# A graph network's gathered rows and one-hots in fp32: two products a tile instead of six, and 56 columns instead of 64

## The chip, the cores and the metric

The kernel runs on one core of one Trainium2 chip. The metric is the device time of one execution in microseconds. Three runs of the kernel before are shown, and one more that was taken with the hardware profiler.

## The reference

The kernel computes two relational graph convolutions over 6250 nodes with 256 features and 206250 edges, then a choice of a linear layer by node type, then a mixture of experts. What the change touches is the first part, twice:

```python
W = jnp.einsum('rb,bde->rde', comp, basis)      # 8 relations from 4 bases
h = jnp.einsum('nd,rde->nre', x, W)
msg = h[src, edge_type]
seg = dst * R + edge_type                        # R = 8
sums = segment_sum(msg, seg, n * R)
cnt = segment_sum(ones, seg, n * R)
agg = (sums / max(cnt, 1)).reshape(n, R, -1).sum(axis=1)
return agg + x @ root + bias                     # relu behind it
```

The edges come sorted by their destination. The input of the first layer is the layer norm of x. Behind the second layer stand `x + lin_w[node_type] ...`, a second layer norm, and 8 experts (256 to 512 to 256, GELU, the two best of eight weighted by a softmax), added to x.

## The kernel before, in words

The kernel does not multiply each edge's message by W. It sums the source rows of each (node, relation) first and multiplies the sums afterwards. A block is 64 nodes, which is 512 (node, relation) columns; there are 98 blocks, 49 pairs. The edges of a block are cut into 18 tiles of 128 (TILES). For a tile, POOL gathers the 128 source rows from a table in DRAM into a slot (L558, an indirect DMA, one slot for each of the 18 tiles), DVE makes a one-hot of each edge's column (L929), and TensorE multiplies the gathered rows (stationary, 128 x 128) by the one-hot (moving) into PSUM banks S[0] and S[1], one for each half of the 256 features (L1251). In the first layer a product of ones by the one-hot counts the edges of each column in bank C (L1247).

**Three parts.** To keep fp32 accuracy with bf16 products the tables hold each row as three bf16 numbers (PARTS = 3: a rounded value, the rounded remainder, and the remainder of that), so a row has 3 x 256 bf16 values, 1536 bytes, and a tile needs 2 halves x 3 parts = 6 products. The one-hot and the ones are bf16, too. Making the parts is work of its own. In the setup, group_parts (L793 to L797) on DVE and a copy on ACT (L636) make them for the first table, in 7 groups of 7 x 128 nodes; store_group on SP (L389 to L395) writes them. In the first layer, save (L955 to L960) on DVE and publish (L669 to L678) on ACT make them for the second table, from the transposed result in T2.

**Columns of a tile.** As the edges are sorted, a tile's edges fall in a few neighbouring nodes. A tile writes SPAN = 8 nodes, COLS = 64 columns, from its base on. The base is the tile's first node, but no more than the base of the tile before plus COLS and no more than TOP = 512 - COLS (L818 to L821). Bases travel to TensorE packed four to a word (L1237 to L1243). If an edge falls outside its tile's columns, `general_i` is set (L842 to L861) and a general path is run instead, which takes 128 edges a step, 1612 steps a layer, with an indirect gather and an indirect adding scatter in each.

**Order of the work.** Everything is written out by hand, engine by engine, with semaphores.

- Setup: SP loads the edges and x in groups (load_group, L347); DVE finds the windows, makes statistics (group_stats, L770), ACT normalizes (norm_group, L622: seven operations L630, then the rounding L636), TensorE transposes each group (turn_group, L1139) and ACT copies it to featT (L643). POOL starts its gathers when all stores of the first table have landed (L603, L604).
- Layer 1: POOL gathers tile after tile, for all pairs; each third tile it waits until TensorE has released the slots (`used`, L569). TensorE takes a block's 18 tiles; after an even block it runs transform of the pair before (L1269: 20 fp32 products of root and bases), after an odd block turn (L1288: 2 transposes, 4 fp32 products). DVE divides by the counts and scales (scale, L933), mixes the bases (mix_bases, L901), makes the next one-hots, and saves. A block's first tile waits for the scaling of the block before (sc_ready, L1220).
- Between the layers: POOL waits until all of the second table has landed (L613).
- Layer 2: TensorE's stream is one list, dense() (L1356), which interleaves the experts of pair r (up, L1338; down, L1351), transform and typed products (L1311, L1312) of pair a, and the tiles of pair y's second block and pair x's first block, one or two tiles at a place. A product of the router (L1328) has 8 columns.

A fp32 product is one call in the code and shows as two matmul records in the trace, each with a weight load; a bf16 product, and a transpose, is one.

Of the kernel before, what the change touches and what calls it, by code (L numbers as in the profile page):

```python
# [14 lines left out]
P = 128  # L15
# [22 lines left out]
PARTS = 3  # L38
# [8 lines left out]
SPAN = 8  # L47
# [21 lines left out]
def build(nc, x, src, dst, etype, ntype, basis0, comp0, root0, bias0, basis1, comp1, root1, bias1,  # L69
          lin_w, lin_b, gamma, beta, Wr, br, W1, b1, W2, b2, out):  # L70
    with ExitStack() as ctx:
# [12 lines left out]
        table = [dram("table0", (NPAD, PARTS * D), BF16), dram("table1", (NPAD, PARTS * D), BF16)]  # L84
# [9 lines left out]
        slot = sb("slot", [P, TILES, PARTS * D], BF16)  # L94
# [18 lines left out]
        ones_b = sb("ones_b", [P, P], BF16)  # L113
# [10 lines left out]
        parts = sb("parts", [P, PARTS, D], BF16)  # L124
        rest = sb("rest", [P, D], F32)
# [25 lines left out]
        def carve(t, at, n):  # L151
            return t[:, at:at + n]
# [3 lines left out]
        grest = carve(ffn_w, 4 * GW, GW).rearrange("p (t d) -> p t d", t=GROUP)  # L156
        gparts = [carve(ffn_w, 5 * GW + i * PARTS * GW // 2, PARTS * GW // 2).bitcast(BF16).rearrange(
            "p (t q d) -> p t q d", t=GROUP, q=PARTS) for i in range(2)]
# [6 lines left out]
        early = slot[:, :, :].rearrange("p t d -> p (t d)").bitcast(F32)  # L165
# [6 lines left out]
        idx_all = carve(ffn_w, 5 * GW + PARTS * GW, BLOCKS * TILES).bitcast(I32).rearrange(  # L172
# [23 lines left out]
        g_rows = carve(early, 3 * MW, PARTS * D // 2).bitcast(BF16)  # L196
        g_sum = carve(early, 3 * MW + 384, MCOLS)
        same = carve(early, 3 * MW + 648, P // 2).bitcast(BF16)
# [57 lines left out]
        g_hi = sem("g_hi")  # L256
        g_rest = sem("g_rest")
        g_mid = sem("g_mid")
        g_lo = sem("g_lo")
# [15 lines left out]
        rest_done = sem("rest_done")  # L275
        mid_done = sem("mid_done")
        lo_done = sem("lo_done")
        parts_out = sem("parts_out")
# [59 lines left out]
        def _(sp):  # L338
# [3 lines left out]
            for q in (sc_ready, relu_done, rest_done, b2_added, mid_done, lo_done, znT_done, lin_acc, feat_saved, *used.values()):  # L342
                sp.sem_inc(q, START)
# [162 lines left out]
            with sp.If(general):  # L506
                sp.wait_ge(parts_out, 16 * PAIRS)
                general_sums(1)
# [977 lines left out]
```

## Time and profile before

| | us |
|---|---|
| median of 3 runs | 4842.9 (4841.66 to 4844.88) |
| the profiled execution | 4840.02 |
| its span, first to last instruction | 4838.2 |
| mean granted TensorE clock, share of full | 0.782 |
| TensorE busy | 3842.3 (79%) |
| TensorE weight loads busy | 3300.8 (68%) |
| DVE busy | 3017.5 (62%) |
| ACT busy | 881.8 (18%) |
| POOL busy | 3331.7 (69%) |

The span holds setup up to about 178 us, layer 1 up to about 2360 us and layer 2 with the experts after it. A busy share is the part of the span in which an instruction of the engine was running; an engine at 69% can still be the one that sets the pace, if the rest is its own time between instructions ("issue"). Matmuls overlap, so their pace is read from start to start and not from the duration of one. The granted clock has two levels, 1.2 GHz (0.5) and 2.4 GHz (1.0).

### The profile page before, as it was taken

How to read it: one execution, taken by the hardware profiler on the slowest of the kernel's cores; microseconds unless marked ns; L12 is line 12 of the kernel's file. 1: busy time of each engine (PE TensorE's matmuls, PEld its weight loads, DVE VectorE, ACT ScalarE, POOL GpSimd, SP SyncE). 2: the span in 40 equal slices, each digit the busy share in tenths (PEclk: the TensorE clock that was granted, in tenths of full speed). 3: DMA queues.
4: the chain of work that ended last, by engine and by line, in shares of the span. 5: the costliest groups of instructions: out<-in, count | busy, mean ns of one | idle time of the engine just before them, and what ended most of it. 6: DMA issues, size and time to landing. Idle time of an engine off the chain costs nothing.

```text
span 4838.2 us, 119647 instructions
## 1 busy us (share of the span) xinstructions
PE 3842.3 (79%) x38119; PEld 3300.8 (68%) x38120; DVE 3017.5 (62%) x6579; ACT 881.8 (18%) x2470; POOL 3331.7 (69%) x3374
## 2 busy tenths in 40 slices
PE   1366666666666666666469999999999999999999
PEld 1255555555555555555358888888888888888888
DVE  4556656666666566666456666666666666666663
ACT  1200000000000000000013333333333333333333
POOL 0477777777777777777477676767676777676770
PEclk6555555555555555555569999999999999999999
DMA  4656655555555555555465555555555555555551
GB/s 129 192 171 183 176 158 156 157 158 158 155 157 159 156 157 158 158 156 157 117 169 166 156 159 155 158 154 158 154 158 156 158 157 160 154 160 154 159 158 22
DMA packets 344661, 749.10 MB, mean 155 GB/s; under 512 B 128323, under 2 KB 167806, under 8 KB 344430
## 3 DMA queue, kind: packets, MB, share of 16 engines
q0 software_dynamic: 215040, 662.09, 48.7%
q1 hardware_dynamic: 115510, 70.49, 5.6%
q10 hardware_dynamic: 14076, 16.04, 1.0%
q8 instruction: 23, 0.38, 0.0%
q14 instruction: 12, 0.10, 0.0%
HBM read 719.00 MB, written 29.35 MB: 155 GB/s over the span
## 4 chain that ended last, share of the span: by engine, by line
PE 59%; issue 12%; DVE 12%; POOL 9%; DMA 8%; DVEq 0%; SPq 0%; ACT 0%; POOLq 0%; ACTq 0%
PE bank L1351 15%; PE bank L1338 14%; PE bank L1251 11%; POOL slot L558 9%; PE bank L1283 8%; DMA slot<-table,idx 6%; DVE inv L939 4%; PE bank L1247 3%; DVE scaled L945 3%; PE bank L1311 3%; PE bank L1312 2%; DVE mixed L913 2%; PE bank L1279 1%; DVE inv L938 1%; PE bank L1314 1%
## 5 line engine op out<-in xcount | busy, mean ns | idle before, releaser
L558 POOL DMA_INDIRECT slot<-table,idx x3354 | 3326.0, 992 | 1342.0 <-issue 1085.2
L1251 PE MATMUL bank<-hot,slot 128*128 (+1 forms) x21168 | 1380.1, 212 | 67.5 <-DMA slot<-table,idx 60.6
L1251 PEld LDWEIGHTS bank<-hot,slot 128*128 128x128 bf16 x21168 | 1112.1, 108 | 219.4 <-issue 75.0
L1247 PE MATMUL bank<-hot,ones_b 128*128 x1764 | 398.7, 226 | 745.4 <-DMA slot<-table,idx 340.1
L1338 PE MATMUL bank<-xnT,ffn_w 128*128 128x128 f32 x6272 | 867.1, 285 | 20.0 <-DVE scaled L945 20.0
L1247 PEld LDWEIGHTS bank<-hot,ones_b 128*128 128x128 bf16 x1764 | 181.0, 103 | 1006.4 <-issue 969.2
L1351 PE MATMUL bank<-ffn_w,act 128*128 128x256 f32 x3136 | 842.0, 395 | 0.3 <-DVE o L1024 0.3
L1338 PEld LDWEIGHTS bank<-xnT,ffn_w 128*128 128x128 f32 x6272 | 755.8, 192 | 46.4 <-DVE scaled L945 28.8
L1351 PEld LDWEIGHTS bank<-ffn_w,act 128*128 128x128 f32 x3136 | 541.1, 191 | 60.7 <-issue 16.9
L913 DVE SCALAR_TENSOR_TENSOR mixed<-scaled,small,mixed 128x256 f32<-128x256 f32 x1372 | 573.7, 480 | 12.2
L913 DVE SCALAR_TENSOR_TENSOR mixed<-scaled,comp_sb,mixed 128x256 f32<-128x256 f32 x1372 | 573.5, 480 | 10.5
L938 DVE TENSOR_SCALAR inv<-bank 128x512 f32<-128x512 f32 x98 | 67.5, 688 | 778.9 <-PE bank L1251 778.9
L691 ACT ACTIVATE act<-bank,small 128x128 f32<-128x128 f32 x1568 | 442.9, 373 | 582.1 <-PE bank L1338 580.9
L1283 PE MATMUL bank<-mixed,basis_sb 128*128 128x128 f32 x3136 | 474.7, 311 | 0.0
L1283 PEld LDWEIGHTS bank<-mixed,basis_sb 128*128 128x128 f32 x3136 | 454.2, 228 | 0.0
L945 DVE TENSOR_TENSOR scaled<-bank,inv 128x512 f32<-128x512 f32 x392 | 377.5, 1040 | 65.8 <-PE bank L1251 52.4
L939 DVE RECIPROCAL inv<-inv 128x512 f32<-128x512 f32 x98 | 328.6, 3353 | 3.4
L1024 DVE SCALAR_TENSOR_TENSOR o<-bank,wfull,o 128x256 f32<-128x256 f32 x343 | 164.5, 480 | 250.3 <-PE bank L1351 245.2
L929 DVE TENSOR_TENSOR hot<-iota_b,rel 128x1152 bf16<-128x1152 bf16 x196 | 264.8, 1352 | 47.1 <-DMA off<-off_d 31.8
L665 ACT ACTIVATE hcur<-bank,small 128x128 f32<-128x128 f32 x98 | 30.7, 364 | 1120.7 <-PE bank L1283 1029.3
L691 ACT ACT_TABLE_LOAD x96 | 123.2, 1283 | 348.4 <-DVE o L1024 347.5
L988 DVE SCALAR_TENSOR_TENSOR x<-bank,tmask,x 128x256 f32<-128x256 f32 x196 | 94.8, 484 | 128.2 <-PE bank L1312 128.2
(148 smaller groups left out, 2192.0 us busy)
## 6 DMA issues: line engine op xcount, KB each, us to landing
slot<-table,idx POOLq DMA_INDIRECT x3354, 3.1
inv<-inv_d SPq DMA_DIRECT2D x98, 256.0 KB, 3.8
table<-ffn_w SPq DMA_DIRECT2D x7, 1344.0 KB, 6.0
table<-parts ACTq DMA_DIRECT2D x49, 192.0 KB, 3.1
ffn_w<-in_L_ffn_W_dram SPq DMA_DIRECT2D x16, 512.0 KB
xcur<-in_x_dram SPq DMA_DIRECT2D x48, 128.0 KB
out_dram<-o ACTq DMA_DIRECT2D x48, 128.0 KB
ffn_w<-in_x_dram SPq DMA_DIRECT2D x6, 896.0 KB, 9.0
```

The costliest lines, as they stand in the source:

```text
L558: gp.indirect_dma_start(out=slot[:, k, :], out_offset=None, in_=table[layer], in_offset=bass.IndirectOffsetOnAxis(ap=idx[:, h, k:k + 1], a ...
L691: last = sc.activation(act[:, e % 2, c, :], HP[e % 2][:, c * P:(c + 1) * P], ACT.Gelu, bias=b1_sb[:, e * HCH + c:e * HCH + c + 1])
L913: ins = v.scalar_tensor_tensor(out=mixed[:, b, :, :], in0=scaled[:, :, r, :], scalar=s, in1=mixed[:, b, :, :], op0=ALU.mult, op1=ALU.add)
L929: v.tensor_tensor(hot[:, h, :, :], iota_b[:, :].unsqueeze(1).broadcast_to([P, TILES, COLS]), rel[:, h, :].unsqueeze(2).broadcast_to([P, TI ...
L939: ch.link(v.reciprocal(iv, iv))
L945: last = v.tensor_tensor(scaled[:, k, :, h * BD:(h + 1) * BD].rearrange("p r n -> p n r"), S[k][:, :].rearrange("p (n r) -> p n r", r=R), ...
L1024: v.scalar_tensor_tensor(out=o[:, :], in0=YP[e % 2][:, 0:D], scalar=wfull[:, 0, e:e + 1], in1=acc[:, :], op0=ALU.mult, op1=ALU.add).then_i ...
L1247: t.matmul(C[:, at], ones_b[:, :], oh, start=(k == 0), stop=(k == TILES - 1), skip_group_check=True)
L1251: last = t.matmul(S[f][:, at], slot[:, k, q * D + f * P:q * D + (f + 1) * P], oh, start=(k == 0 and q == 0), stop=(k == TILES - 1 and q == ...
L1283: last = t.matmul(T[:, o_ * P:(o_ + 1) * P], basis_sb[:, b, k, o_ * P:(o_ + 1) * P], mixed[:, b, k, :], start=(layer == 1 and n == 1), sto ...
L1338: last = t.matmul(HP[e % 2][:, c * P:(c + 1) * P], w1_sb[:, e, k, c * P:(c + 1) * P], xnT[:, k, :], start=(k == 0), stop=(k == HALVES - 1))
L1351: last = t.matmul(YP[e % 2][:, 0:D], act[:, e % 2, c, :], w2_sb[:, e, c, :], start=(c == 0), stop=(c == HCH - 1))
```

## The change

The tables hold plain fp32 rows of 256 values (1024 bytes), and the gathered rows, the one-hots and the ones are fp32. A tile needs one product a half, two in all, and the count product in layer 1. Nothing is split into parts any more: group_parts goes, with ACT's rounding, the store waits for the norm alone and sends xn; save loses its two subtractions, publish is one copy. The norm waits on ACT for the landing of the store two groups before, ahead of its seven operations and no longer behind them. turn waits for `hi_done` (ACT has copied T2) and not for the remainder. SPAN is 7, so a tile has 56 columns and TOP is 456.

```diff
-PARTS = 3
-SPAN = 8
+SPAN = 7
...
-        table = [dram("table0", (NPAD, PARTS * D), BF16), dram("table1", (NPAD, PARTS * D), BF16)]
+        table = [dram("table0", (NPAD, D), F32), dram("table1", (NPAD, D), F32)]
...
-        slot = sb("slot", [P, TILES, PARTS * D], BF16)
+        EARLY = TILES * 384
+        early = sb("early", [P, EARLY], F32)
+        slot = early[:, 0:TILES * D].rearrange("p (t d) -> p t d", t=TILES)
...
-        iota_b = sb("iota_b", [P, COLS], BF16)
+        iota_c = sb("iota_c", [P, COLS], F32)
-        hot = sb("hot", [P, 2, TILES, COLS], BF16)
+        hot = sb("hot", [P, 2, TILES, COLS], F32)
...
             def store_group(i, g):
-                sp.wait_ge(g_hi, g + 1)
-                sp.wait_ge(g_mid, g + 1)
-                sp.wait_ge(g_lo, g + 1)
+                sp.wait_ge(g_norm, g + 1)
...
-                sp.dma_start(dst_ap, gparts[i].rearrange("p t q d -> p t (q d)")).then_inc(g_out[i], 16)
+                sp.dma_start(dst_ap, xn[i]).then_inc(g_out[i], 16)
...
                     act_.wait_ge(g_Tc, g - 1)
-                    act_.wait_ge(g_rest, g - 1)
+                    act_.wait_ge(g_out[i], 8 * (g - i))
...
-                act_.wait_ge(g_norm, g + 1)
-                if not isinstance(g, int) or g >= 2:
-                    act_.wait_ge(g_out[i], 8 * (g - i))
-                sc.activation(gparts[i][:, :, 0, :], xn[i], ACT.Copy).then_inc(g_hi, 1)
...
             def publish(p):
                 act_.wait_ge(hT_done, p + 1)
-                act_.wait_ge(parts_out, p * 16)
-                sc.activation(parts[:, 0, :], T2[:, 0:D], ACT.Copy).then_inc(hi_done, 1)
-                act_.wait_ge(rest_done, START + p + 1)
-                sc.activation(parts[:, 1, :], rest[:, :], ACT.Copy).then_inc(mid_done, 1)
-                act_.wait_ge(lo_done, START + p + 1)
-                act_.wait_ge(mid_done, START + p + 1)
+                act_.wait_ge(rows_out, p * 16)
+                sc.activation(turned[:, :], T2[:, 0:D], ACT.Copy).then_inc(hi_done, 1)
+                act_.wait_ge(hi_done, START + p + 1)
...
-            def group_parts(i, g):
-
-                dve.wait_ge(g_hi, g + 1)
-                if not isinstance(g, int) or g >= 1:
-                    dve.wait_ge(g_lo, g)
-                v.tensor_tensor(grest, xn[i], gparts[i][:, :, 0, :], ALU.subtract).then_inc(g_rest, 1)
-                dve.wait_ge(g_rest, g + 1)
-                v.tensor_copy(gparts[i][:, :, 1, :], grest).then_inc(g_mid, 1)
-                dve.wait_ge(g_mid, g + 1)
-                v.tensor_tensor(gparts[i][:, :, 2, :], grest, gparts[i][:, :, 1, :],
-                                ALU.subtract).then_inc(g_lo, 1)
...
                               ROOTED[:, 0:D].rearrange("p (k n) -> p k n", k=HALVES)).then_inc(feat_saved, 1)
-                dve.wait_ge(hi_done, p + 1)
-                dve.wait_ge(mid_done, START + p)
-                dve.wait_ge(lo_done, START + p)
-                v.tensor_tensor(rest[:, :], T2[:, 0:D], parts[:, 0, :], ALU.subtract).then_inc(rest_done, 1)
-                dve.wait_ge(mid_done, START + p + 1)
-                v.tensor_tensor(parts[:, 2, :], rest[:, :], parts[:, 1, :], ALU.subtract).then_inc(lo_done, 1)
...
                     if self.layer == 0:
-                        t.matmul(C[:, at], ones_b[:, :], oh, start=(k == 0), stop=(k == TILES - 1),
+                        t.matmul(C[:, at], ones_f[:, :], oh, start=(k == 0), stop=(k == TILES - 1),
                                  skip_group_check=True)
                     for f in range(HALVES):
-                        for q in range(PARTS):
-                            last = t.matmul(S[f][:, at],
-                                            slot[:, k, q * D + f * P:q * D + (f + 1) * P], oh,
-                                            start=(k == 0 and q == 0), stop=(k == TILES - 1 and q == PARTS - 1),
-                                            skip_group_check=True)
+                        last = t.matmul(S[f][:, at], slot[:, k, f * P:(f + 1) * P], oh, start=(k == 0),
+                                        stop=(k == TILES - 1), skip_group_check=True)
...
             def turn(p):
                 pe.wait_ge(relu_done, START + p + 1)
-                pe.wait_ge(rest_done, START + p)
+                pe.wait_ge(hi_done, START + p)
```

The rest of the diff renames (`parts_out` to `rows_out`), drops the buffers and semaphores of the parts, and does the same to the general path. It is left out.

## Rows read from the trace of the kernel before

**Rows 1.** Windows of both layers: busy us (instructions) by engine, granted clock, DMA share, GB/s.

```profile
178.00:2360.00 2182.00, 1442.28 (x14748) 1162.54 (x14748) 1365.36 (x2166) 68.05 (x191) 1658.98 (x1674) 0.58 0.57 160
2510.00:4800.00 2290.00, 2269.75 (x22347) 2030.09 (x22345) 1480.19 (x3981) 741.56 (x2108) 1572.33 (x1586) 1.00 0.55 153
```

**Rows 2.** Groups by line, 1000 to 2000 us: busy us, mean ns, idle before.

```profile
L558 POOL DMA_INDIRECT slot<-table,idx x772 | 765.0, 991 | 235.2 <-issue 202.9 <-PE bank L1251 27.4 <-DMA off<-off_d 4.9
...
L1247 PE MATMUL bank<-hot,ones_b 128*128 x810 | 183.0, 226 | 326.3 <-DMA slot<-table,idx 143.1 <-DVE scaled L945 88.3 <-issue 77.5
```

**Rows 3.** Timeline of TensorE, layer 1: start us, us, line, operation.

```profile
1064.07 0.66 PE L1292 MATMUL bank<-ident,hcur 128*128 128x128 f32 x2
...
1506.11 0.66 PE L1292 MATMUL bank<-ident,hcur 128*128 128x128 f32 x2
...
1512.37 0.23 PE L1247 MATMUL bank<-hot,ones_b 128*128 x1 [3.89 <-DVE scaled L945]
...
1528.07 1.92 PE L1283 MATMUL bank<-mixed,basis_sb 128*128 128x128 f32 x8
1529.78 0.49 PE L1279 MATMUL bank<-featT,root_sb 128*128 x2
1530.10 1.06 PE L1283 MATMUL bank<-mixed,basis_sb 128*128 128x128 f32 x8
1530.99 0.39 PE L1279 MATMUL bank<-featT,root_sb 128*128 x2
```

**Rows 4.** Timeline of TensorE, layer 2.

```profile
3016.49 1.89 PE L1351 MATMUL bank<-ffn_w,act 128*128 128x256 f32 x8
3018.22 0.51 PE L1328 MATMUL bank<-wr_sb,xnext 128*128 128x8 f32 x4
3018.66 0.38 PE L1329 MATMUL bank<-br_sb,ones_f 1*128 1x8 f32 x2
3018.97 1.16 PE L1338 MATMUL bank<-xnT,ffn_w 128*128 128x128 f32 x8
3019.97 0.34 PE L1251 MATMUL bank<-hot,slot 128*128 128x64 bf16 x6
3020.14 1.14 PE L1338 MATMUL bank<-xnT,ffn_w 128*128 128x128 f32 x8
3021.11 0.51 PE L1251 MATMUL bank<-hot,slot 128*128 128x64 bf16 x12
3021.46 1.11 PE L1351 MATMUL bank<-ffn_w,act 128*128 128x256 f32 x4
3022.41 0.34 PE L1251 MATMUL bank<-hot,slot 128*128 128x64 bf16 x6
```

**Rows 5.** Windows of one pair in layer 1, cut where the clock changed.

```profile
1489.02:1495.85 6.83, 5.57 (x75) 4.62 (x75) 2.02 (x2) 0.63 (x2) 5.37 (x5) 1.00 0.51 142
1495.85:1533.40 37.55, 24.67 (x246) 19.86 (x245) 26.50 (x44) 0.80 (x2) 28.65 (x30) 0.55 0.57 160
```

**Rows 6.** Groups by line, whole run: a gather in the setup.

```profile
L553 POOL DMA_INDIRECT slot<-key_d,start_i x1 | 1.0, 972 | 10.1 <-DVE start_i L807 10.1
```

**Rows 7.** Timeline of DVE and ACT, setup.

```profile
108.48 0.42 DVE L776 BATCH_NORM_STATS2 gstats<-ffn_w 128x6 f32<-128x256 f32 x1 [3.96 <-issue]
...
149.06 0.42 DVE L776 BATCH_NORM_STATS2 gstats<-ffn_w 128x6 f32<-128x256 f32 x1 [0.66 <-issue]
...
156.65 1.70 ACT L636 ACTIVATE ffn_w<-ffn_w 128x1792 bf16<-128x1792 f32 x1
...
163.30 2.03 DVE L797 TENSOR_TENSOR ffn_w<-ffn_w 128x1792 bf16<-128x1792 f32 x1
```

**Rows 8.** Chain that ended last, in order of time, setup: start us, us.

```profile
165.41 5.51 DMA table<-ffn_w
```

More of the change, by code:

```diff
@@ L123, in build @@
         hcur = sb("hcur", [P, HALVES, P], F32)
-        parts = sb("parts", [P, PARTS, D], BF16)
-        rest = sb("rest", [P, D], F32)
+        turned = sb("turned", [P, D], F32)
         xcur = sb("xcur", [P, D], F32)
@@ L195, in build @@
         zeros = carve(early, 2 * MW, MW)
-        g_rows = carve(early, 3 * MW, PARTS * D // 2).bitcast(BF16)
+        g_rows = carve(early, 3 * MW, D)
         g_sum = carve(early, 3 * MW + 384, MCOLS)
-        same = carve(early, 3 * MW + 648, P // 2).bitcast(BF16)
+        same = carve(early, 3 * MW + D, P)
         below = carve(early, 3 * MW + 712, P)
@@ L274, in build @@
         hi_done = sem("hi_done")
[L275 to L278, printed above, removed]
+        rows_out = sem("rows_out")
         inv_out = sem("inv_out")
@@ L341, in _ @@
             sp.sem_inc(out_done, 16 * START)
-            for q in (sc_ready, relu_done, rest_done, b2_added, mid_done, lo_done, znT_done, lin_acc, feat_saved, *used.values()):
+            for q in (sc_ready, relu_done, hi_done, b2_added, znT_done, lin_acc, feat_saved, *used.values()):
                 sp.sem_inc(q, START)
@@ L607, in _ @@
                 general_sums(0)
-                gp.wait_ge(parts_out, 16 * PAIRS)
+                gp.wait_ge(rows_out, 16 * PAIRS)
                 general_sums(1)
@@ L862, in _ @@
             v.memset(idle[:, :], 0.0).then_inc(tables_ready, 1)
-            group_parts(0, 0)
             ch0 = ch.n - 2 * GL
@@ L869, in _ @@
                     group_stats(i, g2 * 2 + i)
-                    group_parts(1 - i, g2 * 2 + i - 1)
             ch.begin(ch0 + GL * (GROUPS - 1))
             group_stats(0, GROUPS - 1)
-            group_parts(1, GROUPS - 2)
-            group_parts(0, GROUPS - 1)
             general = is_general(dve)
@@ L1189, in general_sums @@
                     pe.wait_ge(edge_rows, n * 16 + 16)
-                    t.matmul(T2[:, D:MCOLS], same, ones_b[:, 0:1], start=True, stop=True)
-                    for q in range(PARTS):
-                        last = t.matmul(T2[:, 0:D], same, g_rows[:, q * D:(q + 1) * D], start=(q == 0),
-                                        stop=(q == PARTS - 1))
+                    t.matmul(T2[:, D:MCOLS], same, ones_f[:, 0:1], start=True, stop=True)
+                    last = t.matmul(T2[:, 0:D], same, g_rows, start=True, stop=True)
                     last.then_inc(edge_sum, 1)
@@ L1246, in tile @@
                     if self.layer == 0:
-                        t.matmul(C[:, at], ones_b[:, :], oh, start=(k == 0), stop=(k == TILES - 1),
+                        t.matmul(C[:, at], ones_f[:, :], oh, start=(k == 0), stop=(k == TILES - 1),
                                  skip_group_check=True)
                     for f in range(HALVES):
-                        for q in range(PARTS):
-                            last = t.matmul(S[f][:, at],
-                                            slot[:, k, q * D + f * P:q * D + (f + 1) * P], oh,
-                                            start=(k == 0 and q == 0), stop=(k == TILES - 1 and q == PARTS - 1),
-                                            skip_group_check=True)
+                        last = t.matmul(S[f][:, at], slot[:, k, f * P:(f + 1) * P], oh, start=(k == 0),
+                                        stop=(k == TILES - 1), skip_group_check=True)
                     if k % RUN == RUN - 1:
```

22 lines of the change are left out of this document (6 added, 16 removed).

## The prediction

> **What bounds the kernel now.** I read the windows first, to cut the run into its stages, then the waits inside each, then the order of TensorE's work at the scale of one tile. Layer 1 (178 to 2360 us) and layer 2 (2510 to 4800 us) have different limits [rows 1]. In layer 1 TensorE is busy 1442 of 2182 us at a mean granted clock of 0.58, in layer 2 for 2270 of 2290 us at 1.00. So layer 2 is TensorE's: whatever is added to its stream there is added to the time.
>
> In layer 1 the engine that is always at work is POOL. Over 1000 us it issued 772 gathers; each shows 991 ns, and of the 235 us between them 203 end in "issue", that is, in nothing but its own sequencer; 27 us are waits for TensorE. TensorE meanwhile waits for gathered rows or for DVE (326 us ahead of the count product L1247) [rows 2]. A gather each 1.25 us is POOL's pace, and a pair of blocks (some 34 gathers) takes 44.2 us: (1506.11 - 1064.07) / 10 from one turn (L1292) to the tenth after it [rows 3].
>
> **What one product costs.** This decides the case, so I read it from start to start in the timeline. At full clock a bf16 tile of layer 2 is six products of 64 columns, and from its first one to the next dense product is 3020.14 - 3019.97 = 0.17 us: 0.029 each. Twelve take 0.35 us. There is a hidden bill behind them: the four records L1351 after a double tile take 3022.41 - 3021.46 = 0.95 us where their own pace, 1.73 us for eight (L1351, 3016.49 to 3018.22), makes it 0.87 [rows 4]; so each switch from tile to dense costs 0.08 more, since there are no long columns left to load fp32 weights behind. A tile alone thus costs 0.25 us, a double one 0.43.
>
> An fp32 product is two records in this trace, each with a weight load of its own. Its pace with 128 columns is 0.89 / 8 = 0.111 us at full clock (L1283, 1530.10 to 1530.99) [rows 3]. The row that bears on the change is L1328: fp32 weights of 128 by 128, and only 8 columns. Its four records still need 3018.66 - 3018.22 = 0.44 us, 0.110 each [rows 4]. So from 8 to 128 columns the weight load sets the pace and the columns cost nothing; 56 columns lie in between. Cutting the span from 64 to 56 columns then buys TensorE nothing. At the half clock the same 128-column record takes (1529.78 - 1528.07) / 8 = 0.214 us [rows 3], and I take a weight-bound record to double likewise.
>
> The six bf16 loads at 0.029 us each are what the old form has going for it. The Trainium skill, "TensorE: Matmul & The Clock Gate", section on LDWEIGHTS, prices any load by its columns alone, at 1.2 a nanosecond. By that estimate six loads of 128 would cost 0.64 us a tile and four 0.43, and layer 2 would win 36 x 0.21 x 46.5 = 350 us. The rows have 0.17 us for the six, so the measurement decides. The page's own next section exempts weights that are not fp32, and that exemption is what the change gives up.
>
> **Part by part.**
>
> Layer 2, tiles: six bf16 records become four fp32 ones: 4 x 0.110 = 0.44 us, and the next dense weight load is already one of the intervals counted. A single tile gains 0.44 - 0.25 = 0.19 us, a double one 0.88 - 0.43 = 0.45 us. By the calls in dense() a pair has 31 places: 26 single, 5 double (18 tiles in the block y, 18 in the block x). 26 x 0.19 + 5 x 0.45 = 7.2 us a pair; 46 loop passes and about half a pair after them: 46.5 x 7.2 = **+335 us**, all on the path, as TensorE has no idle time there. Lower bound: the columns' pace (see the third rival), -51 us. An upper end from loads and columns not overlapping is excluded by the 128-column rows.
>
> Layer 1, tiles: seven records become six (count, S0, S1, two each). The trace of before has no such stream, so I bound it. At half clock a tile takes 6 x 0.214 = 1.28 us, 36 tiles 46.2 us; transform's 40 records 8.6 us; and from the turn to the next block's first tile TensorE waits for DVE's division and scaling, 1512.37 - 1506.11 = 6.3 us, with turn inside [rows 3]. Together 61.1 us, more than POOL's 44.2: TensorE would become the bound here too. Each microsecond at full clock takes one off. Now the clock is full for 6.83 us a pair, after transform's run, then 37.55 us mostly at half, while the engine waits between tiles [rows 5]. If that stays, a pair takes 61.1 - 6.8 = 54.3 us. If the clock is full for 17 us or more, POOL binds again at 44.2, as all 36 tiles at full need only 36 x 0.66 = 23.8 us. What the clock does in a backlog of weight-bound products, where the engine never waits but streams its 56 columns in 56/128 of the time that a record of 128 takes, no row shows. It lies between the two things that rows do show: transform, columns without a break, after which the clock rose, and tiles with waits, after which it fell. I take the middle, 49.3 us, with full clock for 11.8 us: +5.1 x 48 pairs = **+245 us**; bounds 0 and +10.1 x 48 = +485.
>
> POOL's gathers move 1024 bytes a row, not 1536. I book nothing: the gather of 98 rows of 9.2 KB took 972 ns, that of 128 rows of 1.5 KB 991 [rows 2, 6], so bytes do not set it. The DMA share of 0.57 [rows 1] falls, which no one waits for.
>
> Setup: group_parts (three DVE operations of 2 us a group) and ACT's rounding copy go. Groups come 10.15 us apart now, (149.06 - 108.48) / 4. Without the parts a group is statistics, ACT's seven normalizing operations, transposes and copies in a ring, near 9 us; I take 1 us for each of four intervals. Behind the last group ACT begins its rounding at 156.65 with the norm done, yet the last part ends at 165.33 [rows 7]; that store can leave 8.7 us earlier, and its 5.51 us transfer [rows 8] shrinks by a third of its bytes, 1 us. Sum **-13 us**; bounds -18 and -5. ACT's norm now waits for the store of two groups before, ahead of seven operations, and the root of the next group and the featT copies queue behind it; that store is issued a whole group earlier and lands in 5.5, so nothing is booked. On SP the store waits for the norm alone and is sent sooner, ahead of the next loads, which also share the DMA engines: that is in the -5.
>
> Save and publish lose two DVE operations, an ACT one and their waits; turn waits for the copy out instead of the remainder. All lie beside POOL's stream, except once between the layers, less than two gathers' time: nothing booked. One-hots in fp32 have an eighth fewer columns on DVE, which is busy 1365 of 2182 us in layer 1 [rows 1]: nothing.
>
> **Sum.** 4838.2 - 13 + 245 + 335 = 5405; the profiled execution lies 1.8 us over its span (4840.0) and 2.9 under the median: 5410 us.
>
> **Rivals.**
>
> First, the clock in layer 1 stays as it is, 6.8 us a pair: 5410 + 240 = 5650 us. For it: the array is less in use per microsecond than in transform; the clock has fallen after every pair. Chance 0.3.
>
> Second, a TensorE that never waits gets the full clock until its backlog is gone: layer 1 keeps POOL's pace, 5410 - 245 = 5165 us. For it: both stretches after which it fell have waits for rows; layer 2 never loses it. Chance 0.28. The skill's same page, section on the clock gate, has it that activity releases a throttle that is the default; by it this rival's 5165 would come out, if loading weights counts as activity, which it does not say.
>
> Third, the other sign: the weight load of the second record is hidden, and 56 columns go at the columns' pace, (0.216 - 0.111) / 128 us a column, 0.052 us a record. A tile then takes 0.21 us with no switch bill: 0.04 less single, 0.01 less double, 1.1 us a pair, -51 us; layer 1 stays POOL's; with setup 5410 - 245 - 335 - 51 = 4779 us. It decides from 0.0625 us a record down (0.25 / 4). Against it: L1328's 0.110 with 8 columns. Chance 0.04. That page's table of back-to-back gaps would put up to 64 columns at its issue floor; the section warns that pairs of load and product go by both.
>
> Fourth, it does not do what it says: with 7 nodes an edge falls outside its tile's window and the whole kernel takes the general path, 1612 steps a layer with gathers and sums one behind another, tens of milliseconds. Counted over the reference's edges, the largest column any tile needs is 55 of 56 and all 206250 are matched. Under 0.01.
>
> **Chances.** Forecast 0.36, first 0.3, second 0.28, third 0.04, rest 0.02. The range goes from just under the second to just above the first: 5140 to 5690. A measurement of this kernel tells about 0.2% from no change; faster 0.04, same 0.01, slower 0.95.
>
> **What would show it.** Records of L1251 in layer 2 0.11 us apart, four to a tile, and a pair 7 us longer: right; 0.05 apart: the third. In layer 1 POOL's waits for TensorE instead of 27 us in a thousand: the first or the forecast, and the granted clock of the stretch tells them apart (about 0.56 for the first, 0.62 for mine, 0.69 and no waits for the second). Setup right if the first gather starts some 13 us earlier. An L558 much under 991 ns would prove my POOL term wrong.

## The result, and the profile after

The changed kernel takes 5568.9 us (median of 4 runs, 5534.9 to 5618.4) where the kernel before took 4843.9 beside it (4841.7 to 4845.9): a ratio of 1.147 (1.141 to 1.154), for which the highest run, over 1.5% above the lowest, is left out. The profiled execution of after is 5553.33 us, its span 5551.1, which is 712.9 us more than the span of before. The page of after has these two rows, of busy time and of the granted clock in 40 slices:

```profile
PE 5097.1 (92%) x32827; PEld 4895.5 (88%) x32828; DVE 2906.6 (52%) x6460; ACT 850.9 (15%) x2414; POOL 3313.7 (60%) x3373
...
PEclk7566665666666566676669999999999999999999
```

TensorE is busy 92% instead of 79%, though it has fewer records (32827 instead of 38119). The windows of after, for layer 1, for layer 2 and for 1000 us of layer 1 (columns as in [rows 1]), say in which stage TensorE sets the pace:

```profile
165.00:2800.00 2635.00, 2345.47 (x13108) 2310.11 (x13107) 1336.51 (x2113) 49.52 (x147) 1657.19 (x1695) 0.64 0.32 91
2900.00:5520.00 2620.00, 2602.98 (x18935) 2449.68 (x18934) 1461.02 (x3979) 738.95 (x2101) 1567.88 (x1574) 1.00 0.33 93
1000.00:2000.00 1000.00, 902.85 (x4993) 890.27 (x4993) 515.50 (x817) 19.16 (x57) 633.14 (x644) 0.63 0.31 88
```

In layer 1 TensorE went from 1442 of 2182 us busy [rows 1] to 2345 of 2635. Against [rows 2] the waits in the groups of 1000 to 2000 us have turned round:

```profile
L543 POOL DMA_INDIRECT early<-table,idx x644 | 633.1, 983 | 363.8 <-issue 181.1 <-PE bank L1203 179.3 <-DMA off<-off_d 3.4
L1203 PE MATMUL bank<-hot,early 128*128 x2696 | 622.1, 376 | 0.0
...
L1200 PE MATMUL bank<-hot,ones_f 128*128 x1347 | 378.0, 377 | 96.5 <-DVE scaled L906 95.5 <-issue 0.4
```

POOL issues 644 gathers instead of 772 and waits 179 us for TensorE where it waited 27. TensorE waits for gathered rows no more, only for DVE's scaling. A gather of 1024-byte rows shows 983 ns, one of 1536 bytes 991: bytes did not set it.

**Layer 2, one tile.** The timeline of TensorE after, in the stretch that answers to [rows 4], and the router's row over the whole run for both kernels (first and last of 49 pairs' calls):

```profile
3083.24 0.51 PE L1278 MATMUL bank<-wr_sb,xnext 128*128 128x8 f32 x4
...
3084.00 1.16 PE L1288 MATMUL bank<-xnT,ffn_w 128*128 128x128 f32 x8
3084.99 0.55 PE L1203 MATMUL bank<-hot,early 128*128 128x56 f32 x4
3085.38 1.12 PE L1288 MATMUL bank<-xnT,ffn_w 128*128 128x128 f32 x8
3086.33 1.00 PE L1203 MATMUL bank<-hot,early 128*128 128x56 f32 x8
3087.16 1.09 PE L1301 MATMUL bank<-ffn_w,act 128*128 128x256 f32 x4
3088.09 0.55 PE L1203 MATMUL bank<-hot,early 128*128 128x56 f32 x4
```

```profile
L1278 PE MATMUL bank<-wr_sb,xnext x196: 172/256/382, 2863.6 to 5503.1; 128*128 128x8 f32 x196
```

```profile
L1328 PE MATMUL bank<-wr_sb,xnext x196: 172/256/383, 2486.5 to 4789.8; 128*128 128x8 f32 x196
```

From a single tile to the next place is 3086.33 - 3084.99 = 1.34 us, where it was 3021.11 - 3019.97 = 1.14 [rows 4]: 0.20 more. Round the double tile, 3088.09 - 3086.33 = 1.76 against 3022.41 - 3021.11 = 1.30: 0.46 more. A pair is (5503.1 - 2863.6) / 48 = 54.99 us against 47.99. Below, "a pair of layer 2" is always this quotient. It is a mean over 48 steps; the router's starts show that the last of them takes 39.7 us in both kernels and most others 55.35 us against 48.10, which is 7.25 more.

**Layer 1, the clock.** TensorE's timeline after, round two turns:

```profile
1519.97 0.33 PE L1200 MATMUL bank<-hot,ones_f 128*128 x2
...
1520.58 0.39 PE L1200 MATMUL bank<-hot,ones_f 128*128 x2
...
1521.25 0.39 PE L1200 MATMUL bank<-hot,ones_f 128*128 x2
...
1532.60 0.41 PE L1242 MATMUL bank<-ident,hcur 128*128 128x128 f32 x2
...
1539.14 0.67 PE L1200 MATMUL bank<-hot,ones_f 128*128 x2 [5.24 <-DVE scaled L906]
...
1540.45 0.63 PE L1200 MATMUL bank<-hot,ones_f 128*128 x2
...
1541.73 0.63 PE L1200 MATMUL bank<-hot,ones_f 128*128 x2
...
1616.30 1.06 PE L1233 MATMUL bank<-mixed,basis_sb 128*128 128x128 f32 x8
1618.31 0.42 PE L1200 MATMUL bank<-hot,ones_f 128*128 x2 [0.95 <-DVE scaled L906]
```

And the windows of after: two whole pairs, each from its transform on (the one between them takes 49.39), then the stretches at one clock of each:

```profile
1512.87:1562.21 49.34, 44.05 (x267) 43.56 (x268) 27.24 (x43) 1.01 (x3) 32.86 (x34) 0.71 0.32 91
...
1611.60:1669.10 57.50, 52.32 (x267) 51.80 (x268) 27.07 (x43) 1.01 (x3) 34.66 (x36) 0.56 0.29 83
```

```profile
1518.30:1538.80 20.50, 15.55 (x135) 15.05 (x133) 7.94 (x8) 1.01 (x3) 12.24 (x13) 1.00 0.30 83
1538.80:1566.10 27.30, 26.96 (x126) 26.97 (x127) 17.79 (x36) 0.00 (x0) 20.90 (x22) 0.50 0.34 98
1613.80:1620.70 6.90, 5.95 (x52) 5.72 (x51) 5.17 (x4) 0.63 (x2) 2.80 (x3) 0.99 0.28 77
1620.70:1671.90 51.20, 46.97 (x221) 46.68 (x221) 22.44 (x40) 0.38 (x1) 32.46 (x33) 0.50 0.30 84
```

A tile takes 1521.25 - 1520.58 = 0.67 us at 2.4 GHz and 1541.73 - 1540.45 = 1.28 at 1.2 GHz, six records at the paces of [rows 3]. There are two kinds of pairs. In the short one the clock rises in transform, lasts through the first block behind it (block A) and is gone when the wait of 5.24 us behind the turn ends; the second block (B) runs at half clock, 23.1 us of tiles without a break (1539.14 to 1562.21), and so do the first 3.9 us of the next transform. TensorE is busy 26.96 us of these 27.30. In the long one it is full for 6.9 us and falls inside block A. I sorted 47 pairs by the step from the start of transform's last record to the start of block A's first tile. The last record itself is 0.27 us of it, so the idle time is 0.27 less. In 28 pairs the step is 0.11 to 0.74 us and they take 49.5 on average, in 15 it is 0.82 to 1.28 and they take 57.2; the other 4, at 0.65 to 0.77, take 54.2. What ends the step is DVE's scaling:

```profile
1513.21 0.69 DVE L899 TENSOR_SCALAR inv<-bank 128x512 f32<-128x512 f32 x1 [9.12 <-PE bank L1203]
1513.93 3.35 DVE L900 RECIPROCAL inv<-inv 128x512 f32<-128x512 f32 x1
1517.32 1.94 DVE L906 TENSOR_TENSOR scaled<-bank,inv 128x512 f32<-128x512 f32 x2
```

DVE begins its division as transform begins, and has scaled 1519.26 - 1512.87 = 6.4 us later; in the long pair the first tile comes after 1618.31 - 1611.60 = 6.7. Transform needs 8.6 us at half clock and about half of that at full: where the clock rises early in it, TensorE is done first, waits about 1 us for DVE, and the full clock ends a few tiles later. The clock record of the trace has it so: it rises 3.3 to 5.5 us into transform in the 28 pairs and 2.2 to 3.1 us into it in the 15. As the early rise and the longer wait always come together here, the pairs alone can't tell which of the two ends the clock; that was put to the test below.

**The account of the 712.9 us.** First gather 17.1 us earlier; from it to the first transform 71.2 -> 87.6 us, 16.4 later; layer 1's pair 44.38 -> 52.23 on average, times 48: +377.3; from the last transform of layer 1 to the first router +0.5; from there to the last router, (5503.1 - 2863.6) - (4789.8 - 2486.5) = +336.2; the tail -0.4. Sum 712.9.

The setup's part shows in POOL's and TensorE's timelines and in the chain after:

```profile
156.31 0.97 POOL L543 DMA_INDIRECT early<-table,idx  x1 [96.98 <-issue]
```

```profile
161.52 0.67 PE L1200 MATMUL bank<-hot,ones_f 128*128 x2 [8.76 <-DMA early<-table,idx]
...
191.19 0.67 PE L1200 MATMUL bank<-hot,ones_f 128*128 x2 [6.38 <-DVE scaled L906]
```

```profile
149.48 4.39 DMA table<-ffn_w
```

The groups come 8.2 us apart, not 10.15 (DVE's first statistics of a group start at 108.56 and, four groups on, at 141.39), and the store takes 4.39 us for 5.51 [rows 8]. But three blocks are summed before the first transform, and both kernels have the half clock there. Before, TensorE was busy 32 of the 66.6 us up to that transform; after, 70 of the 82.4, as a tile takes 1.28 us. That gives the gain back.

### The profile page after: what moved, and what is told of

Same layout as the page of the kernel before. It is cut to its first block, busy times and chain, and to the rows that moved or that the text cites. A ratio compares the mean times of both kernels' runs of the same rounds, so it can differ in the third digit from the quotient of the medians.

```text
span 5551.1 us, 108722 instructions
## 1 busy us (share of the span) xinstructions
PE 5097.1 (92%) x32827; PEld 4895.5 (88%) x32828; DVE 2906.6 (52%) x6460; ACT 850.9 (15%) x2414; POOL 3313.7 (60%) x3373
## 4 chain that ended last, share of the span: by engine, by line
PE 85%; DVE 9%; issue 3%; DMA 1%; POOL 1%; ACT 0%; DVEq 0%; POOLq 0%; SPq 0%; ACTq 0%
PE bank L1203 35%; PE bank L1301 13%; PE bank L1288 12%; PE bank L1200 12%; PE bank L1233 6%; DVE inv L900 4%; DVE scaled L906 3%; PE bank L1261 2%; PE bank L1262 2%; DVE inv L899 1%; PE bank L1229 1%; PE bank L1264 1%; PE bank L1360 1%; POOL early L543 1%; DMA early<-in_src_dram 0%
## 5 line engine op out<-in xcount | busy, mean ns | idle before, releaser
L543 POOL DMA_INDIRECT early<-table,idx x3354 | 3308.1, 986 | 2068.0 <-issue 1126.7
L1203 PE MATMUL bank<-hot,early 128*128 (+1 forms) x14112 | 2578.2, 320 | 26.2 <-DMA early<-table,idx 17.3
L1203 PEld LDWEIGHTS bank<-hot,early 128*128 128x128 f32 x14112 | 2456.7, 241 | 79.1 <-issue 28.4
L1200 PE MATMUL bank<-hot,ones_f 128*128 x3528 | 975.7, 372 | 264.0 <-DVE scaled L906 252.9
L1200 PEld LDWEIGHTS bank<-hot,ones_f 128*128 128x128 f32 x3528 | 812.2, 283 | 296.5 <-issue 286.0
L1233 PE MATMUL bank<-mixed,basis_sb 128*128 128x128 f32 x3136 | 460.9, 305 | 0.0
L1233 PEld LDWEIGHTS bank<-mixed,basis_sb 128*128 128x128 f32 x3136 | 441.5, 222 | 0.0
L890 DVE TENSOR_TENSOR hot<-iota_c,rel 128x1008 f32<-128x1008 f32 x196 | 235.4, 1201 | 46.9 <-issue 29.0
```

Of the source, the lines that this page charges most:

```text
L543: gp.indirect_dma_start(out=slot[:, k, :], out_offset=None, in_=table[layer], in_offset=bass.IndirectOffsetOnAxis(ap=idx[:, h, k:k + 1], a ...
L890: v.tensor_tensor(hot[:, h, :, :], iota_c[:, :].unsqueeze(1).broadcast_to([P, TILES, COLS]), rel[:, h, :].unsqueeze(2).broadcast_to([P, TI ...
L1200: t.matmul(C[:, at], ones_f[:, :], oh, start=(k == 0), stop=(k == TILES - 1), skip_group_check=True)
L1203: last = t.matmul(S[f][:, at], slot[:, k, f * P:(f + 1) * P], oh, start=(k == 0), stop=(k == TILES - 1), skip_group_check=True)
L1233: last = t.matmul(T[:, o_ * P:(o_ + 1) * P], basis_sb[:, b, k, o_ * P:(o_ + 1) * P], mixed[:, b, k, :], start=(layer == 1 and n == 1), sto ...
```

## The experiments

Each is timed against the kernel before on the same chip (medians 4837.5 to 4839.4; 4843.9 beside after, so in a comparison with after's 5568.9 up to 6 us belong to the chip). The first six take the fp32 kernel apart, the last six ask which part of the change was worth having.

**Span 8 in the fp32 kernel**, 64 columns a tile.

```diff
-SPAN = 7
+SPAN = 8
```

> The changed kernel with SPAN back at 8: 64 columns of 128 in each fp32 product, everything else as changed. Theory W (an fp32 record goes at the pace of its weight load, whatever its columns up to 128): layer 2's stretch at full clock stays 2662 us within 0.3%, and a tile in layer 1 stays 1.28 us at half clock. Rival (the columns add to the load, (0.216 - 0.111) / 128 us each): 8 columns more add 0.007 us a record, 4 x 36 x 46.5 x 0.007 = +44 us in layer 2. For the clock, theory K (how much the array streams columns decides whether the full clock lasts until the next block's wait): with 64 columns it lasts in more pairs, all periods go to 49.4 us instead of the mix of 49.4 and 57.3, and the time falls by up to 2.8 x 48 = 134 us, to about 5430. Rival K2 (loading weights counts as much): no difference in layer 1, about 5565 us.

Measured: 5575.9 us, ratio 1.151 (1.149 to 1.153), the same as after. The router's row:

```profile
L1278 PE MATMUL bank<-wr_sb,xnext x196: 172/256/382, 2906.2 to 5545.4; 128*128 128x8 f32 x196
```

A pair of layer 2 is 54.98, after 54.99: the cut of the columns was worth nothing in fp32, as its weight loads set the pace. Layer 1 kept its mixture: 24 pairs of 49.4 us with a step of 0.92 or less, 23 of 57.6 with 1.00 or more. An even 49.4 did not come.

**Span 10 in the fp32 kernel**, 80 columns.

```diff
-SPAN = 7
+SPAN = 10
...
-        EARLY = TILES * 384
+        EARLY = 6400
```

> The changed kernel with SPAN 10, 80 columns, and the shared setup buffer cut to what is used so that it fits. Theory W: layer 2 still 2662 us. Rival (columns add): 24 columns more than 56, 0.020 us a record, +134 us in layer 2. Theory K: at least as much full clock in layer 1 as with 64 columns, so no period over 50 us, 5430 us or less. Rival K2: the mix of periods stays, about 5565 us.

Measured: 5479.0 us, ratio 1.132 (1.130 to 1.135). Layer 2's pair is 55.03, still unmoved, at 43% more columns than after. Layer 1 was quicker, 50.5 us a pair: only 7 of 48 were long (58.3 us), those with a step of 1.57 us or more, while 21 with steps of 0.79 to 1.09 stayed short. Neither forecast for layer 1 came: not all pairs are short, and the old mixture is gone. So the tile time is the same, but steps that gave long pairs in after (from 0.82 us) gave short ones here: the wait alone does not decide. How the columns come into it, these runs do not settle.

**The count product once a block** (its results, the counts, are left out: one product of ones by 512 columns stands for 18).

```diff
-                    if self.layer == 0:
-                        t.matmul(C[:, at], ones_f[:, :], oh, start=(k == 0), stop=(k == TILES - 1),
-                                 skip_group_check=True)
+                    if self.layer == 0 and k == 0:
+                        t.matmul(C[:, :], ones_f[:, :], root_sb[:, 0, :, :].rearrange("p k d -> p (k d)"),
+                                 start=True, stop=True)
```

> The changed kernel whose count product (two records in each tile of layer 1) is replaced by a single product of ones by 512 columns of the root matrix for each block, so the division is by other numbers and the counts are left out. Theory (layer 1 is bound by TensorE's weight loads): a tile takes 4 x 0.214 = 0.86 us at half clock, less than POOL's 1.25, so layer 1 goes back to POOL's 44.2 us a pair, -8.0 x 48 = -385 us: about 5185 us, with layer 2 at 2662. Rival (layer 1 is longer for another reason, such as the wait for DVE or slower gathers): the period stays above 49 us.

Measured: 5119.5 us, ratio 1.058 (1.056 to 1.060), below what was expected. Its window and POOL's group, 1000 to 2000 us:

```profile
1000.00:2000.00 1000.00, 886.46 (x4544) 827.55 (x4543) 621.69 (x985) 23.17 (x69) 760.87 (x786) 0.62 0.38 107
```

```profile
L543 POOL DMA_INDIRECT early<-table,idx x786 | 761.8, 969 | 239.4 <-issue 230.0 <-PE bank L1203 8.8 <-DMA off<-off_d 0.6
```

A pair of layer 1 is 43.5 us, POOL's own pace (1000 / 786 = 1.27 us a gather), at a granted clock no higher than after's. Without two of the six records of a tile the whole +377 is gone; and as the columns make no difference to a record's time, what binds layer 1 of after is TensorE's weight loads.

**28 products behind each turn** (none of their results is read).

```diff
                 last.then_inc(root_ps, 1)
+                for _ in range(28):
+                    t.matmul(bank[6][:, 0:P], ident[:, :], ones_f[:, :], start=True, stop=True)
```

> The changed kernel with 28 fp32 products of ones behind each turn in layer 1, into a bank that nothing reads: at full clock 56 records of 0.111 us fill 6.2 of the 6.5 us in which TensorE waits for DVE's division and scaling. Theory: that wait is what ends the full clock (20.5 us after it rose, in every pair of 49.4 us), so block B runs at full clock too, a pair needs 4.4 + 12.6 + 7 + 12.6 = 37 us of TensorE and falls to POOL's pace of 44 to 46 us: 5170 to 5280 us, layer 2 at 2662. Rival (the clock falls after that time whatever the engine does): the mix of 49.4 and 57 us stays and the filler at half clock runs 12 us, 5.5 more than the wait, so 5800 us.

Measured: 5466.8 us, ratio 1.130 (1.128 to 1.132): faster than after by 100 us with more work, but the expected gain was missed. Its windows (filler, block B and transform, block A) and the first tile of block A:

```profile
1494.80:1498.00 3.20, 3.20 (x32) 3.20 (x30) 3.13 (x10) 0.00 (x0) 0.00 (x0) 1.00 0.00 1
1498.00:1514.40 16.40, 16.40 (x148) 16.31 (x147) 14.75 (x27) 0.00 (x0) 10.60 (x11) 1.00 0.29 79
...
1518.00:1541.24 23.24, 23.24 (x110) 23.24 (x111) 1.87 (x2) 0.38 (x1) 17.38 (x19) 0.50 0.36 102
```

```profile
1516.46 0.42 PE L1200 MATMUL bank<-hot,ones_f 128*128 x2 [1.96 <-DVE scaled L906]
```

The clock now rises in the filler and is full through block B and transform, and it is block A that runs at half. Transform at full clock ends 2 us before DVE, and in that wait the clock falls. I had filled one of two waits and the other took its place.

**Products in both waits**: the 28, and 10 more behind each transform of layer 1.

```diff
                 last.then_inc(tr_done, 1)
+                if layer == 0:
+                    for _ in range(10):
+                        t.matmul(bank[6][:, 0:P], ident[:, :], ones_f[:, :], start=True, stop=True)
```

> The filler kernel with 10 more fp32 products behind each transform of layer 1: at full clock 2.2 us of products in the 2 us in which TensorE still waited there for DVE (the run before, where the full clock ended at that wait and a pair took 50.6 us). Theory (in layer 1 the full clock ends where TensorE waits between blocks, and nothing else ends it while there is a backlog): with both waits filled the clock stays full until the backlog is gone, and a pair goes to POOL's pace, 44 to 46 us: 5150 to 5260 us. Rival (a long stream of weight-bound products ends the full clock by itself): the full clock still ends inside a block, and a pair stays at 49 us or more, over 5400 us.

Measured: 5180.6 us, ratio 1.071 (1.069 to 1.073), as expected.

```profile
1000.00:2000.00 1000.00, 985.08 (x7650) 971.14 (x7648) 603.45 (x949) 22.80 (x68) 766.58 (x767) 0.88 0.37 104
```

```profile
L543 POOL DMA_INDIRECT early<-table,idx x767 | 766.6, 1000 | 233.7 <-issue 203.8 <-PE bank L1203 26.8 <-DMA off<-off_d 3.0
```

38 useless products a pair take 388 us off. Clock 0.88, POOL waits 26.8 us for TensorE as in [rows 2], a pair takes 44.5. Nearly all that is left of the loss, 5180.6 - 4839.4 = 341 us, is layer 2's 336. The clock did not stay full all the time:

```profile
1468.09:1502.23 34.14, 33.90 (x298) 33.43 (x297) 24.26 (x42) 0.62 (x2) 26.22 (x27) 1.00 0.36 102
1502.23:1512.47 10.24, 10.18 (x48) 10.16 (x49) 3.37 (x2) 0.38 (x1) 7.80 (x9) 0.50 0.44 117
```

It fell inside block A, where TensorE had caught up with the gathers and waited for rows again (0.30 us at 1502.29; 27 such waits in 1000 us, the longest 0.5), and it rose again in the filler. This run leaves one rival: the filler takes a wait away and puts 128-column products in its place, so the gain may come from the one or the other.

**Three tiles at a place in fp32** (layer 2's list with 12 places instead of 31; the calls change as in the bf16 kernels further down).

> The changed kernel with the tiles of layer 2 three at a place, 12 places a pair instead of 31. Theory (an fp32 tile leaves no switch to pay for: its records go at the pace of weight loads, and so does the first dense one behind it): a pair of layer 2 stays at 55.35 us within 0.3 us. Rival (the 0.083 us belongs to the place, whatever the type): 19 x 0.083 = 1.6 us less, 53.8 us a pair.

Measured: 5534.4 us, ratio 1.144 (1.142 to 1.146); a pair of layer 2 54.44, 0.55 less, where 0.3 was allowed for. Of this, 0.37 us is a wait of TensorE for DVE's scaling that after has (6.6 us in 18 pairs of 3000 to 4000 us) and this run has not. The rest is 0.01 us for each of the 19 places saved: between fp32 products a switch costs next to nothing.

**Span 7 in the kernel before**, bf16 parts kept.

```diff
-SPAN = 8
+SPAN = 7
```

> The kernel before with SPAN 7 alone: six bf16 products of 56 columns. Theory: nothing to win. Layer 1 is POOL's, and in layer 2 a bf16 record takes 0.029 us where 64 columns at 2.4 GHz are 0.027 and 56 are 0.023; if columns set its pace, 6 x 36 x 46.5 x 0.003 = -30 us (-0.6%); if the weight load or the issue does, no change. I expect within 0.3% of 4843 us.

Measured: 4809.0 us, ratio 0.994 (0.992 to 0.996): the alternative of my expectation, a gain of 0.6%.

```profile
L1328 PE MATMUL bank<-wr_sb,xnext x196: 172/256/381, 2473.2 to 4755.0; 128*128 128x8 f32 x196
```

A pair of layer 2 is 47.54, 0.45 us less. From start to start a bf16 record of a tile takes 26 ns (median) where it took 29, 0.65 us over the 216 of a pair; the waits for DVE's scaling grew by 0.17 us and took part of it back. The half of the change that was of no use in fp32 was the useful half in bf16.

**Three tiles at a place in the kernel before**, to save the switches from bf16 to fp32. Core of the edit, in dense():

```diff
-                ups(1, (1, 2))
+                ups(1, (0, 3))
...
-                downs(0, (1, 1))
-                ups(2, (1, 1))
-                downs(1, (1, 1))
+                downs(0, (0, 3))
+                ups(2)
+                downs(1, (0, 3))
...
-                    if j < TYPES:
-                        more(1)
+                    if j in (1, 3):
+                        more(3)
```

> The kernel before with the tiles of layer 2 taken three at a place, 12 places a pair instead of 31, all else as before. Theory (each place where bf16 tiles go over to fp32 products costs TensorE 0.083 us, an fp32 weight load that no long columns cover): 19 x 0.083 = 1.6 us a pair, x 46.5 = -73 us, about 4766 us. Rival (the cost is the loads' own, or three tiles at once wait for their rows): no change or slower, at or over 4839.

Measured: 4801.0 us, ratio 0.992 (0.991 to 0.994), a gain half the size expected. The waits of 3000 to 4000 us (us in total, times, longest), in the kernel before and in this one, name what took the rest:

```profile
PE bank L1338 <- DVE scaled L945: 8.6, 20, 0.4
```

```profile
PE bank L1338 <- DVE scaled L945: 20.8, 21, 1.0
```

The pair of layer 2 went from 47.99 to 47.14, and the wait in it grew from 0.43 to 0.99 us. Without that the gain would be 0.85 + 0.56 = 1.41 us, 0.07 for each of the 19 places, near the 0.083 expected. Block y is opened one expert behind the last tiles of block x, and waits for DVE to scale x's sums.

**The two together**: span 7 and three at a place, by both edits above.

> The same with SPAN 7, 56 columns, which alone gave 0.994 (-30 us). Theory: the two add up, since the one shortens records and the other removes switches: 4839 - 73 - 30 = 4736 us. Rival (layer 2 comes near POOL's pace and stops gaining): not under 4760.

Measured: 4765.4 us, ratio 0.985 (0.983 to 0.987). The parts add: 0.6% and 0.8% give 1.5%. The forecast was 4736; what it falls short by is the same wait, now 25.2 us in 22 pairs, 1.15 each. The time is the rival's (not under 4760), but the rival's reason, POOL's pace, is not what holds it.

**Six at a place, span 7**: 6 places.

```diff
-                ups(1, (1, 2))
+                ups(1, (0, 6))
...
-                downs(1, (1, 1))
+                downs(1, (0, 6))
```

> The same with six tiles at a place, 6 places a pair. Theory: 25 switches less than before, 2.1 us a pair, -97 us, with SPAN 7 -127: 4712 us; a pair then takes 45.6 us, still over POOL's 43 to 44. Rival (six tiles at once run ahead of the gathers, one each 1.25 us, and TensorE waits for rows or POOL for slots): slower than three at a place.

Measured: 4942.9 us, ratio 1.022 (1.020 to 1.024), a miss with the wrong sign. The waits of 3000 to 4000 us, and the timeline where six tiles stand in a row:

```profile
PEld bank L1251 <- issue: 57.8, 157, 0.7
```

```profile
3003.92 1.12 PE L1251 MATMUL bank<-hot,slot 128*128 128x56 bf16 x30
3005.37 0.36 PE L1251 MATMUL bank<-hot,slot 128*128 128x56 bf16 x6 [0.33 <-issue]
```

After 30 records at a stretch TensorE waits for nothing but its own instructions ("issue"). Not for rows, as the rival had it. My reading, which no run tests: each tile's columns are found at run time by instructions in TensorE's own stream, and that work was hidden beside the dense products between the tiles, while a bf16 tile has only 0.17 us on the array to hide it behind.

**The last tiles of block x a half-step earlier**, else as the two together.

```diff
-                ups(7)
+                ups(7, (0, 3))
...
-                downs(7, (0, 3))
+                downs(7)
```

> The bf16 kernel with SPAN 7 and three tiles at a place, with the last three of block x moved from the last place of the list to one half-step earlier, so that DVE's scaling of that block is done before the next block is opened. Theory: the 1 us a pair in which TensorE waited there (PE waits for DVE's scaled, 25 us in 1000) goes, 46.8 to 45.8 us a pair, -46 us on 4765: about 4720 us. Rival (POOL's pace, 34.2 gathers and block overheads, takes over): not under 4750.

Measured: 4766.4 us, ratio 0.985 (0.984 to 0.986), no gain. DVE and TensorE at the wait:

```profile
3058.25 1.02 DVE L945 TENSOR_TENSOR scaled<-bank,inv 128x512 f32<-128x512 f32 x1
...
3059.32 0.71 PE L1338 MATMUL bank<-xnT,ffn_w 128*128 128x128 f32 x4 [1.25 <-DVE scaled L945]
```

TensorE waits as long as before, 1.25 us here and 27.7 us in 22 pairs, against 25.2: the scaling ends at 3059.27 and TensorE goes on at 3059.32. I read it as DVE's order of work holding the scaling back; then what must move is the consumer.

**Block y opened later, behind transform**, on top of the one above (the lines removed are those of the kernel before).

```diff
                 ups(0)
-                more = open_block(y, 1)
-                ups(1, (1, 2))
+                ups(1)
                 if a is not None:
                     transform(1, a + PAIRS, a)
-                downs(0, (1, 1))
-                ups(2, (1, 1))
+                more = open_block(y, 1)
+                downs(0, (0, 3))
+                ups(2, (0, 3))
```

> The bf16 kernel with SPAN 7 and three tiles at a place, where the block y is opened behind the second up product and transform instead of ahead of it. Moving the last tiles of block x alone did nothing (4766 against 4765): the trace shows DVE's order, expert 6, one-hots, then the scaling that ends 59.27, and TensorE waits 1.25 us a pair at the opening. Theory: 1.8 us of up products and transform's 4.4 us in between cover it, so the pair goes from 46.8 to 45.5 us, -58 us: about 4708 us. Rival (POOL's pace takes over): not under 4740.

Measured: 4695.2 us (4692.9 to 4696.6), ratio 0.971 (0.969 to 0.972), as expected. Its window of layer 2 and its router:

```profile
2510.00:4600.00 2090.00, 2090.00 (x21839) 1905.66 (x21838) 1427.95 (x3880) 713.95 (x2030) 1557.50 (x1575) 1.00 0.59 166
```

```profile
L1328 PE MATMUL bank<-wr_sb,xnext x196: 172/256/383, 2473.5 to 4642.7; 128*128 128x8 f32 x196
```

TensorE has no wait left, busy 2090.00 of 2090, and a pair is 45.19 us. This kernel beats both: it takes 2.9% less time than the one before and 15.7% less than the one changed.

## Why the prediction was right, and where it was off

The forecast was 5410 (5140 to 5690), the result 5569. The direction and both places of the loss were right; the term of layer 1 was too small by 132 us, and a gain in the setup did not come through.

**What one product costs: right.** The row of 8 columns, 0.110 us a record, was the row to read. Tiles of 56, 64 and 80 columns gave pairs of 54.99, 54.98 and 55.03 us. The third rival (columns' pace) is gone: the records lie 0.111 us apart (median of after in 3000 to 4000 us), but for the second of a tile, which comes 0.05 behind the first.

**Layer 2: +335 forecast, +336.2 measured.** Single tiles +0.19 forecast and +0.20 found, double ones 0.45 and 0.46; 7.2 us a pair forecast, 7.25 found in most. The switch bill of 0.08 that was credited to the old form exists, once the waits for DVE are counted: three at a place gave 0.85 us of pair and 0.56 of added wait over 19 places, 0.07 each, in bf16 and 0.01 in fp32. In the last kernel, which also lost the 0.60 us of wait that the span-7 kernel has (12.6 us in 21 pairs), it is (47.54 - 45.19 - 0.60) / 19 = 0.09.

**Setup: -13 forecast, -17.1 measured, and worth nothing.** The step that failed is what was left out: the sum took the gain straight through to layer 1, whose term counts from the first transform on. But the three blocks ahead of that transform go at half clock, at 1.28 us a tile, +16.4 us, where before the tiles waited for rows and were as quick as the gathers.

**Layer 1: +245 forecast, +377 measured.** This term made the miss. Its frame held: 61.1 us a pair at half clock, less somewhat under a microsecond for each that TensorE works at full. The 11.8 us given back, which was taken as a middle, is by chance just what the short pair gets back (61.1 - 49.4 = 11.7): the clock is full for 20.5 us there, and 5.2 of them are the wait. The failed step is that it was one number for all pairs. A third of the pairs are long, and these are worse than the first rival (57.2 against 54.3): part of their 6.9 us of full clock is a wait for DVE. So of 48 pairs the mean is 52.2. The granted clock in 1000 to 2000 us was 0.63, near the 0.62 given as the sign of the forecast, and POOL's waits rose from 27 to 179 us. But the sign is a mean of two kinds, 0.71 in the short pairs and 0.56 in the long one of the windows above, so that it came out is luck, too.

**The second rival's mechanism came true once the waits were filled.** The clock then stayed full until the backlog was gone, 34.1 of 44.4 us, and layer 1 kept near POOL's pace: the time is 5181, against 5165 for the rival. What it had wrong is that after does wait: 5.2 us behind each turn and 0.55 to 1.0 us behind some transforms, both for DVE. The prediction had named the first of these waits in its 61.1 us and not seen that it ends the clock.

**What the clock answers to is not settled.** In after it did not rise in 23.1 us of tiles without a break (block B), though once full it held through the 12.6 us of such tiles in a short pair's block A; it rose in transform and in the filler, products of 128 columns. A step of 1.0 us gave a long pair at 56 and at 64 columns and a short one at 80. The Trainium skill, "TensorE: Matmul & The Clock Gate", section "What's actually happening", says that activity releases a default throttle. If a stream of weight loads counts as activity, the trace of after does not agree: block B would have had the full clock. I ran no kernel that varies only the columns in such a stream with all waits gone, and none that takes the waits away without adding products. Nor was the setup's part tried alone, nor the fp32 kernel with DVE's division made shorter, which would shorten both waits at their source.

## What to carry to other kernels

Before trading several cheap products for one wide-typed product, find in the trace the shortest product of the new kind and read its pace from start to start; where weight loads set it, neither fewer columns nor half as many products helps, and the two parts of such a change should be timed apart, as here one was worth 0.6% and was buried under 15%. Where the granted clock of TensorE changes within a stage, ask for each of its waits what clock stands before and behind it (here the pairs with some 0.5 us more wait took 8 us longer), and try useless work in it before rebuilding the schedule. Count a wait that a change adds or removes apart from what the change itself is worth. Interleaving has a price per switch and a return in hidden issue, so its grain has an optimum (three tiles here, not one or two and not six), and the engine that feeds the place must be checked at each step.

## What the runs showed that I had not expected

- Pairs in which TensorE waited 0.55 to 1.0 us between transform and the tiles took 57 us in place of 49. Runs of one kernel spread over 83 us (5535 to 5618) where the kernel before spreads over 4. The granted clock falls with it, from 0.824 in the shortest run to 0.802 in the longest, which fits a differing number of long pairs; only one of these runs has a trace to count them in.
- 38 products whose results no one reads made the kernel 388 us faster (5569 -> 5181).
- bf16 records of 56 columns come 26 ns apart, those of 64 columns 29; fp32 ones from 8 to 80 columns all take 0.11 us at 2.4 GHz.
- Six bf16 tiles in a row cost TensorE's own issue: 58 us of idle on its weight loads in 1000 us, and 50.4 us a pair against 46.7 with three.
- A gather's time on POOL is 969 to 1000 ns in all kernels, at 1024 and at 1536 bytes a row; halving the DMA share (0.57 to 0.32 in layer 1) bought nothing.
